# New instruction orders at the first batch and at the experts' opening of a two-layer decoder, and three weight splits moved from GpSimd to VectorE

## What is computed

```
h = layernorm(x)
q, k, v = silu(h Wq), silu(h Wk), silu(h Wv)          # 16 heads of 16
o = (q k^T * D) v          # D[h]: exp(-decay * distance), causal, 256 x 256 for each head
o = rmsnorm_per_head(o * sigmoid((h Wg1) Wg2)) * w
x = x + o Wo
x = x + 0.6 * sigmoid(si + sj) + 0.4 * layernorm(x)   # si, sj: two projections of the context
h = layernorm(x)
x = x + shared(h) + sum over the 6 chosen of 16 experts of p_e * (silu(h Wg_e) * (h Wu_e)) Wd_e
```

## Time and profile before

| | us |
|---|---|
| median of 3 runs (lowest to highest) | 925.93 (925.31 to 926.55) |
| the profiled execution, its own time | 926.81 |
| its span, from the first to the last instruction | 924.7 |
| PE busy in the span | 895.0 (97%) |
| PE weight loads | 687.3 (74%) |
| DVE busy | 614.1 (66%) |
| ACT busy | 426.1 (46%) |
| POOL busy | 107.1 (12%) |
| mean granted TensorE clock | 0.994 |

### The profile page before, as it was taken

One profiled execution on the slowest core, in us unless ns is written; L12 is line 12 of the kernel. 1 busy time (PEld: TensorE's weight loads), 2 busy tenths in 40 slices (PEclk: granted clock), 3 DMA queues, 4 the chain that ended last, 5 costly groups with the idle time before them and its releaser, 6 DMA issues.

```text
span 924.7 us, 14203 instructions
## 1 busy us (share of the span) xinstructions
PE 895.0 (97%) x5377; PEld 687.3 (74%) x5377; DVE 614.1 (66%) x1182; ACT 426.1 (46%) x1065; POOL 107.1 (12%) x131
## 2 busy tenths in 40 slices
PE   7997999999999999999999999999999999999998
PEld 4664778888888786667867777777766778888886
DVE  4568756666665757666787687777786566666665
ACT  7364634333433459883344343434344443333342
POOL 4003100000000130001233232323210000000000
PEclk9899999999999999999999999999999999999999
DMA  6004011111100230004500000000010111111001
GB/s 186 1 2 138 14 37 52 35 51 51 51 0 1 84 144 2 2 1 159 191 1 1 1 1 1 1 1 1 1 35 18 35 52 51 44 41 51 17 0 46
DMA packets 12537, 37.10 MB, mean 40 GB/s; under 512 B 2080, under 2 KB 4352, under 8 KB 11712
## 3 DMA queue, kind: packets, MB, share of 16 engines
q1 hardware_dynamic: 12448, 36.32, 11.9%
q0 software_dynamic: 32, 0.01, 0.0%
HBM read 35.27 MB, written 1.05 MB: 39 GB/s over the span
## 4 chain that ended last, share of the span: by engine, by line
PE 84%; DVE 7%; ACT 6%; issue 1%; DMA 1%; SPq 0%; POOL 0%; DVEq 0%; ACTq 0%
PE ps L1334 78%; PE ps L1962 3%; PE ps L1507 2%; ACT Q L1121 1%; DMA X<-in_x 1%; DVE stats L460 1%; DVE xn L468 1%; DVE P L536 1%; ACT whi L1136 0%; ACT silu_g L1161 0%; DVE weighted_h L684 0%; ACT probs_q L1236 0%; ACT h_hi L1166 0%; DVE h_lo L694 0%; DVE probs_q L853 0%
## 5 line engine op out<-in xcount | busy, mean ns | idle before, releaser
L1166 ACT ACTIVATE h_hi<-weighted_h 128x512 fp32r<-128x512 f32 x100 | 63.2, 632 | 154.2 <-DVE weighted_h L684 152.1
L694 DVE TENSOR_TENSOR h_lo<-weighted_h,h_hi 128x512 fp32r<-128x512 f32 x100 | 69.2, 692 | 66.5 <-ACT h_hi L1166 66.3
L1334 PE MATMUL ps<-xT_first,whi 128*128 128x512 f32 x376 | 111.3, 397 | 1.2 <-ACT silu_g L1161 1.2
L1334 PE MATMUL ps<-xT_second,whi 128*128 128x512 f32 x376 | 108.5, 391 | 1.3 <-ACT silu_g L1161 1.2
L720 DVE TENSOR_TENSOR shared_gate<-silu_g,row_shares 128x512 f32<-128x512 f32 x88 | 60.8, 691 | 63.5 <-ACT silu_g L1161 63.4
L1161 ACT ACTIVATE silu_g<-ps 128x512 f32<-128x512 f32 x100 | 59.7, 597 | 78.1 <-PE ps L1334 77.9
L1334 PE MATMUL ps<-xT,merged_q 128*128 128x256 f32 x384 | 91.9, 383 | 0.0
L1326 POOL TENSOR_TENSOR latent_rot<-rope_buf 128x256 f32<-128x256 f32 x96 | 68.5, 734 | 180.2 <-DVE rope_buf L808 180.2
L1334 PEld LDWEIGHTS ps<-xT_first,whi 128*128 128x128 f32 x376 | 70.3, 188 | 19.0 <-issue 2.8
L1334 PEld LDWEIGHTS ps<-xT_second,whi 128*128 128x128 f32 x376 | 70.1, 188 | 17.1 <-issue 2.5
L1334 PE MATMUL ps<-h_hi,wlo 128*128 128x512 f32 x200 | 78.4, 392 | 0.0
(11 more groups left out here) (197 smaller groups left out, 1569.0 us busy)
## 6 DMA issues: line engine op xcount, KB each, us to landing
raw<-in_ffn SPq DMA_DIRECT2D x50, 384.0 KB, 3.0
wx<-in_wx SPq DMA_DIRECT2D x4, 2048.0 KB, 11.1
cx<-in_cx SPq DMA_DIRECT2D x1, 1536.0 KB, 6.6
X<-in_x SPq DMA_DIRECT2D x4, 256.0 KB, 7.3
kvc<-in_kvc SPq DMA_DIRECT2D x1, 1024.0 KB, 14.3
out<-X SPq DMA_DIRECT2D x4, 256.0 KB, 2.2
wqkv<-in_wqkv SPq DMA_DIRECT2D x1, 768.0 KB, 8.5
wqkv<-in_wqkv SPq DMA_DIRECT2D x1, 512.0 KB, 6.8
```

Of the source, the lines that this page charges most:

```text
L694: v.tensor_tensor(h_lo[:, u % 2, :], weighted_h[:, u % 2, :], h_hi[:, u % 2, :].bitcast(F32), ALU.subtract).then_inc(act_lo[l], 1)
L1166: a.activation(h_hi[:, u % 2, :], weighted_h[:, u % 2, :], ACT.Copy).then_inc(act_hi[l], 1)
L1334: return pe.matmul(o, l, r, start=start, stop=stop, skip_group_check=True)
```

## The change

It moves instructions and adds or removes none but loads of ACT's function table; the three low parts that POOL computed are computed by DVE.

1. First batch, PE (a = 0): `keys(1)` and `links(0)` come before `scores_by_key(0, 1)`; `gate_inner(1)` and `links(1)` come between the second and third group of scores, `values(1)` after the third. ACT reads `links(0)` after `gate_inner(1)`.
2. Batches 2 and 3, PE: `output0(a - 2)` comes before `gate(a)`.
3. The low parts of chunks 0, 1 and 2: off POOL, and on DVE at three places: behind `bilinear(1)`, behind `scaled(0, 3)`, and behind the last `normalise(2, 3)`. `scaled(0, 3)` itself comes before `normalise(1, 2)`.
4. ACT: `silu(0, 0, 0)` comes behind `logit_exponentials(0, 0)`, together with the next one, and the table for exp is loaded ahead behind `copy_logits(0, 1)`.
5. Opening of the experts of layer 0: the split of chunk 3 moves from before `router_maxima(0, 1)` into step 3 on ACT and DVE, `router_maxima(0, 1)` comes before `act_low(0, 2, 2)`, and PE transposes the second half's logits before `gate_half(0, 3)` instead of behind it. Layer 1 keeps its order.

```diff
@@ vector, attention0 @@
                 bilinear(NB - 3)
+                v.wait_ge(pe_last_p0, 1)
+                split_lo(0, 0, 0)
                 gated_values(NB - 1)
                 norm_statistics(2, NB - 3)
                 add_out(0, NB - 2)
                 norm_statistics(1, NB - 2)
                 normalise(2, NB - 3)
+                scaled(0, NB - 1)
+                split_lo(0, 1, 1)
                 normalise(1, NB - 2)
-                scaled(0, NB - 1)
                 tokens_low(0, 0)
...
                 normalise(2, NB - 1)
+                split_lo(0, 2, 2)
                 weight_shared(0, 0)
@@ vector, experts @@
                 weight_shared(l, 2)
+                if l == 0:
+                    router_maxima(l, 1)
                 act_low(l, 2, 2)
-                if l == 0:
-                    v.wait_ge(w_lo[0], EARLY)
-                split_lo(l, 3, 3)
-                router_maxima(l, 1)
+                if l == 1:
+                    split_lo(l, 3, 3)
+                    router_maxima(l, 1)
...
                             router_probabilities(l, 1)
+                        if l == 0 and isinstance(n, int) and n == EARLY:
+                            split_lo(l, 3, 3)
                         act_low(l, n, u)
@@ scalar, attention0 @@
-                        if period == 0:
-                            links(0)
...
                         gate_inner(c)
+                        if period == 0:
+                            links(0)
                         values(c)
...
                 tokens_high(0, 0)
-                silu(0, 0, 0)
-                a.preload_act_table_set(LN_EXP)
                 norm(2, NB - 2)
...
                 logit_exponentials(0, 0)
+                silu(0, 0, 0)
                 silu(0, 1, 1)
...
                 copy_logits(0, 1)
+                a.preload_act_table_set(LN_EXP)
@@ scalar, experts @@
                 act_high(l, 2, 2)
-                split_hi(l, 3, 3, 0)
+                if l == 1:
+                    split_hi(l, 3, 3, 0)
...
                         silu(l, n, u)
+                        if l == 0 and isinstance(n, int) and n == EARLY:
+                            split_hi(l, 3, 3, 0)
@@ gpsimd @@
-                if t == 4:
-                    g.wait_ge(pe_last_p0, 1)
-                    for c in range(EARLY):
-                        g.wait_ge(w_hi[0], c + 1)
-                        g.tensor_tensor(wlo[:, c, :], raw[:, c, :], whi_first[:, c, :].bitcast(F32), ALU.subtract).then_inc(w_lo[0], 1)
@@ tensor, attention0 @@
                     scores_by_key(a, 0)
+                    if a >= 2:
+                        output0(a - 2)
                     if a >= 1:
                         gate(a)
-                    if a >= 2:
-                        output0(a - 2)
...
                     if c < NB:
                         queries(c)
+                    if a == 0:
+                        keys(c)
+                        pe.wait_ge(xb_loaded, 16 * 2)
+                        links(0)
                     scores_by_key(a, 1)
-                    if c < NB:
+                    if a == 0:
+                        gate_inner(c)
+                        links(1)
+                    elif c < NB:
                         keys(c)
...
                     scores_by_key(a, 2)
+                    if 1 <= a < NB - 1:
+                        gate_inner(c)
                     if c < NB:
-                        gate_inner(c)
                         values(c)
@@ tensor, experts @@
+                            if l == 0 and isinstance(n, int) and n == EARLY - 1:
+                                logits_by_token(l, 1)
                             gate_half(l, n + 1, i, last, u + 1)
-                            if isinstance(n, int) and n == EARLY - 1:
+                            if l == 1 and isinstance(n, int) and n == EARLY - 1:
                                 logits_by_token(l, 1)
```

7 lines of the change are left out of this document (1 added, 6 removed).

## The result

| | before | changed |
|---|---|---|
| median of 4 runs each (lowest to highest), us | 926.24 (925.31 to 926.64) | 915.25 (914.95 to 915.38) |
| the profiled execution, its span | 926.81, 924.7 | 915.24, 913.5 |
| mean granted TensorE clock | 0.994 | 0.998 |

The ratio is 0.9883 [0.9868, 0.9897]: the change saves 11 us (1.2%).

What follows compares the result with a forecast made beforehand. The prediction took PE as the bound, with 84% of the chain that ended last. Its terms, -5.2 - 0.85 - 1.8 + 0.4 - 1.4 = -8.85 us, took 925.93 to 917.1, range 914.9 to 921.2.

Steps and rivals of the forecast that it cites:

- First batch, -5.2: PE, first batch: keys and links fill the wait for the second score group and the clock stays up, 5.2 us gained.
- the two new waits: First batch, PE: inner gate waits 0.2 us for ACT's keys, third score group 0.2 us for DVE's products.
- the clock's part, 2.7: First batch, PE: with a short gap the clock stays up, so scores and keys together take 2.7 us less.
- Projection before gate, -0.85: Batches 2 and 3, PE: the projection covers batch 3's 0.83 us gate wait for ACT's values; 0.85 us gained.
- POOL's splits gone, -1.8: End of attention, DVE: without POOL's splits, two `on` save 1.45 us and four `xn` 0.4; 1.8 us gained.
- Splits on DVE, `scaled` earlier, silu later, +0.4: DVE, last P to gate 2: splits added, table-load wait gone; gate 2 comes 0.4 us later than other gains put it.
- 0.9 hops + 0.8 root wait: DVE idle time assumed from last P to last `normalise`: 0.9 us norm-to-DVE hops, 0.8 waiting for the last batch's root.
- more is won: Rival: product of squares at full clock (1.0) and first split covered (0.4), gain 10.2, time 915.7; chance 0.09.
- Opening, -1.4: Experts' opening, gate 2 to gate 4: PE's 1.39 us wait for silu 3 goes, stretch takes 11.3 us; 1.4 gained.
- that rival (919.9): Rival: DVE bounds the opening, splits use up the 1.8 and half the 1.4 is lost; 919.9 us, chance 0.18.
- The clock did not fall in the first batch: Rival: the clock falls in the first batch all the same, gain only 6.2 us, time 919.8; chance 0.07.
- The slower case: Rival: new PE gaps of about 1.2 and 0.3 us bring the low clock into the opening, up to 929; chance 0.04.

Runs made afterwards that it cites:

- the changed kernel's second profile: The changed kernel run once more with no edit, as yardstick beside three further variants: 915.35 us, ratio 0.9883.

## Why the prediction was right, and where it was off

**First batch, -5.2: right, in sum and step by step.** Measured 5.01 in place, and again 5.01 with this part alone. The scores wait 0.71 us (0.45 expected) and take 1.15; the two new waits are 0.16 and 0.23 (0.2 and 0.2 expected); the clock's part, 2.7, was 2.66 where the gap was filled with zeros. The scores started at 22.94 and not at 23.35, which is the 0.41 us by which DVE's row ahead of them was earlier. Its P times v came at 32.20 (32.4 expected); in the time of before, with these 0.41 added, that is 32.61, 0.2 late, as the wait for the scores was. The 2.7 of the clock hangs on how long the low level lasts in the execution that one compares with. What I missed is that this part alone keeps only a part of its gain, 4.0 us by the ratio and 2.1 up to gate 2 in its profile: the clock fell at two later places.

**Projection before gate, -0.85: right in place (0.89, and 0.89 lost again when it is taken out), wrong as a price.** I took the gap for its own length. Taken out of the changed kernel it is 2.1 us, put alone into the kernel before it is -1.0 us (its interval just reaches no change). The second difference comes from POOL's splits, which block one `on` or two, depending on 0.9 us, and from the clock behind them; the first fits the clock that may fall behind the gap, in executions without a trace. The prediction priced neither.

**POOL's splits gone, -1.8: right (2.0 to the last P).** `on` took 0.88 for two and the four `xn` 1.37 at this place. By the rule of the Trainium skill that the prediction cites (SBUF - State Buffer, "Who interferes with whom") the new splits on DVE might have met POOL's adds. They did not: the three split rows took 0.96, 0.95 and 0.95 us, and POOL's adds lay beside other work of DVE. The runs agree with the rule in both directions: 3.97 us for two `on` beside POOL, and no loss for DVE's P beside it, one of whose inputs comes from PSUM.

**Splits on DVE, `scaled` earlier, silu later, +0.4: the term that was off.** It measured -1.1, which is 1.5 of the 1.85 us between forecast and time, and lies outside the term's own bound of -0.75 (which its numbers do not give either: 0.4 less 0.95 for the product of squares is -0.55). The step that failed is "0.9 hops + 0.8 root wait": I let DVE's stretch from the last P to the last `normalise` take 18.0 us again, 16.3 of work and 1.7 idle. The work was right (16.08), the idle time was 0.46. I had misread the old idle time. This row of before, which the prediction does not show, has most of what I called hops in one piece:

```profile
91.25 0.74 DVE L468 TENSOR_SCALAR xn<-X,mv,rstd 128x256 f32<-128x256 f32 x2 [1.50 <-ACT rstd L932]
```

The 3.65 us idle were 0.53 ahead of `og`, this 1.50 for the root behind the product of squares, the 1.36 of the table load, and 0.23 at the last root. So there were hardly any hops to pay for, and one root wait that was larger than the 0.8. Of the root wait 0.19 was left, 1.31 less. 0.95 of the 1.31 is the product of squares at full clock (1.13 us, 2.08 in the earlier trace rows), so that `rrec` came as much earlier; the rest is cover by the work moved there. That was my bound, and I had put it with the small chance of "more is won". It is in part luck: in the six profiles of the kernel before and its variants the product took 1.12 to 1.13 in three and 2.07 to 2.08 in three, so the profile of before could have shown either. In seven of the eight profiles of the changed kernel and its variants it took 1.12 to 1.13, in one 1.57. In the changed kernel the root of every other norm is there when DVE gets to it, but for 0.23 at the last one. The first split's cost, 0.43, was 0.25 on the path (the run with it on POOL). The third split did stand ahead of gate 2 as computed: 0.92 us from `normalise` to gate 2, 0.97 expected. Silu's move, taken out of the changed kernel, is worth 0.24 us there, and nothing that the times could tell from noise.

**Opening, -1.4: right (1.54; 1.34 alone).** PE is late next, as said: 11.17 busy of 11.17.

**The rivals.** DVE did become the bound of the stretch before gate 2, but the stretch got shorter, not longer; the price of that rival (919.9) assumed that its idle time was unavoidable. Its price has a slip, too: with half of the 1.4 lost the sum keeps 0.7 of it and not 0.4, which gives 6.35 and 919.6. The clock did not fall in the first batch. "More is won" (915.7) came nearest: its first half, the product of squares at full clock, is what happened. The forecast's own range ended at 915.8, so the measured time is this rival's and not the forecast's. The slower case did not come: the new gap ahead of the last `xn`, 1.2 us in the prediction, was 0.62 us in the changed kernel's second profile (0.49 in the kernel before), and in the opening the clock stayed at 1.00. Its argument against was wrong, though. It said that the low level was seen only behind 1.47 us and more; the runs show it behind 0.83.

**The rest.** 0.4 of the 11.2 us between the two spans lies before anything that was changed. Against the medians (11.0), which have no such part, the ledger's other rows would give 10.8.

## What to carry to other kernels

Price an edit on a full engine by the work it adds and the idle time that it can fill, and ask of each idle microsecond what would still cause it afterwards; to take the old idle time over as a constant was the one wrong term here. Price parts of a change from both ends, alone in the old kernel and taken out of the new one: here the same swap of two calls was worth -1.0 and +2.1 us. A gap on PE may cost more than its length, in some executions only, so compare the clocks of the executions before believing a difference of one or two microseconds. And when two profiles are subtracted, do it stretch by stretch from a row ahead of the change: here the start alone moved by up to 1.25 us, and a clock that fell elsewhere can pass for an edit's gain or loss, as in the profiles of the opening alone and of the first silu early.

## What the runs showed of the hardware

- The granted clock fell to 0.50 behind a gap of 0.83 us on PE in two of the six profiles that have it. The profile of before and that of the changed kernel with the gate first have the gap and 1.99 us or full clock behind it; the first batch alone and the splits alone have the same gap with 3.47 and 3.68 us for the projection. What decides between the two was not found, and no run filled this gap.
- Before varied from 924.37 to 929.72 us over 31 runs, at mean clocks of 0.991 to 0.996; the changed kernel from 914.76 to 916.39 over 8, at 0.997 to 1.000. Part of the gain is that there are fewer gaps behind which the clock can fall. How large that part is cannot be read from one profile: in the two shown it is the 2.7 us of the first batch and the 0.95 of the product of squares.
- GpSimd's subtraction of 128x768 (two inputs from SBUF) beside DVE's `on` (two inputs from SBUF) took 3.94 us for two, against 1.82 for one beside P, while the two `on` took 3.97 against 0.88: DVE pays for the meeting, GpSimd hardly. The same subtraction takes DVE 0.96.
- A low clock beside a busy DVE cost nothing: the stretch to gate 2 took 19.72 us with clock 0.50 at 82 to 84 us and, in three other profiles, without a fall. A fall about 1.5 us earlier, in the product of squares that DVE waits for, cost 0.46.
- A load of ACT's function table took 1.28 us in its row, and in the kernel before the next activation followed 0.02 us behind it (96.53 plus 1.28, next row at 97.83).
